# Self attention of layer 1 in steps of two units, with the transposed probabilities in the banks of the scores

## The reference

```
def cross_attention(x, ctx, wq, wk, wv, wo, bo):      # here ctx is the same layer-normed x
    q = einsum('bne,ef->bnf', x, wq).reshape(B, N, 20, 64).transpose(0, 2, 1, 3)
    k = einsum('bme,ef->bmf', ctx, wk)...; v = einsum('bme,ef->bmf', ctx, wv)...
    attn = softmax(einsum('bhnd,bhmd->bhnm', q, k) * 64 ** -0.5)
    out = einsum('bhnm,bhmd->bhnd', attn, v).transpose(0, 2, 1, 3).reshape(B, N, 1280)
    return einsum('bnf,fe->bne', out, wo) + bo
x = cross_attention(layer_norm(x, g1, be1), layer_norm(x, g1, be1), wq1, wk1, wv1, wo1, bo1) + x
```

## Time and profile before

| | us |
|---|---|
| median of 3 runs | 3640.47 (3639.7 to 3643.22) |
| the profiled execution, its own time | 3640.09 |
| its span in the trace | 3638.3 |
| self attention stage `a1`, first product to the last sum | 1145.08 to 2329.39 |

### The profile page before, as it was taken

The page is one execution under the profiler, slowest core; times in us unless marked ns, Lnnn a source line. Parts: engine busy times, 40 slices in busy tenths (PEclk is TensorE's granted clock), DMA queues, the critical chain, the costliest instruction groups (busy, mean ns, idle before and its releaser), DMA issues. The chain is left out here.

```text
span 3638.3 us, 93033 instructions
## 1 busy us (share of the span) xinstructions
PE 3565.8 (98%) x37535; PEld 3078.2 (85%) x37535; DVE 2316.8 (64%) x3902; ACT 2073.9 (57%) x5150; POOL 1255.6 (35%) x1278
## 2 busy tenths in 40 slices
PE   8999999999998999999999999799999999999999
PEld 6777787878887898989889898688888888888888
DVE  5788866664554666666667676566666666666554
ACT  5777777774335555555555555455555555555333
POOL 5333333331443333333333333322233222333432
PEclk9999999999999999999999999999999999999999
DMA  4444332322001000000000000100000000000000
GB/s 108 104 121 101 94 91 77 93 75 73 0 0 35 2 1 2 2 2 1 2 2 1 2 2 1 25 4 3 4 3 3 4 3 4 3 3 2 20 22 22
DMA packets 99740, 101.44 MB, mean 28 GB/s; under 512 B 31248, under 2 KB 74128, under 8 KB 99344
## 3 DMA queue, kind: packets, MB, share of 16 engines
q1 hardware_dynamic: 93408, 94.41, 10.2%
q0 software_dynamic: 5120, 1.35, 0.2%
q10 hardware_dynamic: 816, 0.08, 0.0%
HBM read 20.76 MB, written 5.24 MB: 7 GB/s over the span
## 5 line engine op out<-in xcount | busy, mean ns | idle before, releaser
L1250 POOL TENSOR_TENSOR a_probs<-a_probs,a_rsums 128x1024 f32<-128x1024 f32 x160 | 303.9, 1899 | 752.1 <-DVE a_rsums L1407 752.1
L1288 ACT ACTIVATE a_probs<-a_scores_banks,a_negmax 128x128 f32<-128x128 f32 x1280 | 367.4, 377 | 284.0 <-DVE a_negmax L1395 284.0
L1288 ACT ACTIVATE c_probs<-c_scores_banks,c_negmax 128x77 f32<-128x77 f32 x1280 | 317.6, 350 | 251.4 <-DVE c_negmax L1395 251.1
L1250 POOL TENSOR_TENSOR c_probs<-c_probs,c_rsums 128x616 f32<-128x616 f32 x160 | 197.8, 1236 | 729.9 <-DVE c_rsums L1407 729.9
L724 ACT ACTIVATE s_probs<-s_scoresT_banks 128x1024 f32<-128x1024 f32 (+1 forms) x320 | 327.6, 1024 | 181.4 <-PE s_scoresT_banks L901 179.2
L810 DVE TENSOR_REDUCE s_negmax<-s_scores_banks 128x8 f32<-128x1024 f32 (+1 forms) x320 | 322.4, 1007 | 135.5 <-PE s_scores_banks L883 131.3
L1388 DVE COPY a_outT<-a_out_bank 128x512 f32<-128x512 f32 x160 | 110.7, 692 | 294.2 <-PE a_out_bank L1605 239.4
L1789 DVE SCALAR_TENSOR_TENSOR f_hidden<-f_value_bank,bias,f_gate 128x512 f32<-128x512 f32 x160 | 120.1, 750 | 247.2 <-ACT f_gate L1764 245.2
L679 POOL DMA_DIRECT2D s_q_stack<-s_shift x160 | 93.8, 586 | 488.0 <-ACT s_shift L747 481.6
L1395 DVE TENSOR_REDUCE a_negmax<-a_scores_banks 128x4 f32<-128x512 f32 x320 | 206.2, 686 | 86.9 <-PE a_scores_banks L1475 86.9
L1764 ACT ACTIVATE f_gate<-f_gate_bank,bias 128x512 f32<-128x512 f32 x160 | 110.1, 688 | 260.6 <-PE f_value_bank L325 260.5
(11 more groups left out here) (306 smaller groups left out, 10405.0 us busy)
## 6 DMA issues: line engine op xcount, KB each, us to landing
s_q_stack<-front SPq DMA_DIRECT2D x192, 160.0 KB, 3.3
s_k_stack<-front SPq DMA_DIRECT2D x96, 160.0 KB, 3.8
s_out<-s_heads SPq DMA_DIRECT2D x128, 80.0 KB, 2.6
s_k_stack<-front SPq DMA_DIRECT2D x96, 96.2 KB, 2.9
x_tokens<-in_x SPq DMA_DIRECT2D x16, 320.0 KB, 3.6
out_x<-x_tokens SPq DMA_DIRECT2D x16, 320.0 KB, 2.4
s_q_stack<-s_shift POOLq DMA_DIRECT2D x160, 8.0 KB, 2.6
s_ctx_in<-in_ctx SPq DMA_DIRECT2D x16, 115.5 KB
```

Of the source, the lines that this page charges most:

```text
L1250: nc.gpsimd.tensor_tensor(probs[i][:], probs[i][:], rsums[(k - 1) % 2][:].unsqueeze(2).broadcast_to([P, UNIT, NK]), ALU.mult).then_inc(s_p ...
L1288: done = nc.scalar.activation(probs[i][:, h, :], scores[:, h // GROUP, h % GROUP * NK:(h % GROUP + 1) * NK], ACT.Exp, bias=negmax[k % 2][: ...
```

## The change

The self attention gets a builder of its own, `attention_wide_self`. Its steps are *doubles* d of two units, first = 2d and second = 2d + 1. The scores of both units are issued together, then everything that uses the full array (Y, P, V, T of both, in a fixed order), then the head outputs of both. There is a second set of score banks, and the transposed probabilities of unit n go into the banks of the scores of the same parity (those of unit n + 2, once its exponentials have been read), so that `pt` is gone; the head outputs of odd units go into `odd_bank`. `probsT` and `outT` have two buffers, `probs` four and not five. The output projection is four units behind and not three. The layer norm's transposes use `even_bank`, and its ScalarE part is split in a scaling (early in the step) and casts (at its end). Cross attention and all else stay as they were. The core of the diff (S, T and O are `scores_step`, `transpose_step` and `values_step`):

```diff
     def scalar_affine(self, e, n, par, bank, parts_used):
+        self.scalar_scale(e, n, bank)
+        self.scalar_high(e, n, par, parts_used)
+
+    def scalar_scale(self, e, n, bank):
         nc, m, t = self.m.nc, self.m, self.t
         if isinstance(n, int) and n == 0:
...
+    def scalar_high(self, e, n, par, parts_used):
+        nc, t, n = self.m.nc, self.t, n + self.offset
         e.wait_ge(t.s_y, n * 2 + 2)
...
+def attention_wide_self(m, tag, wo, context, weights, norm, following, next_norm, crossing):
...
+    T_LAG, Y_LAG = 2, 4
...
+        scores = [banks2(f"scores{i}") for i in range(2)]
+        out_bank, y_bank, even_bank, odd_bank = bank("out"), bank("y"), bank("even"), bank("odd")
...
+        probs = [sb(f"probs{i}", [P, UNIT, TOK]) for i in range(4)]
...
+        probsT = [sb(f"probsT{i}", [P, UNIT, P]) for i in range(2)]
+        outT = [sb(f"outT{i}", [P, GROUP * P]) for i in range(2)]
...
+            for d in range(-3, DOUBLES + 2):
+                step(d, 2 * d, 2 * d + 1)
+                for k in range(2 * d - LAST, 2 * d - LAST + 2):
+                    hand_over(k)
+
...
+            def step(d, first, second):
+                which, ahead, seq = transposed_at(d)
+                exponentials(first, 0, 4)
+                if which:
+                    which.scalar_scale(act, ahead, even_bank)
+                n = context_at(d)
+                if n is not None:
+                    act.wait_ge(crossing.s_T, n + 1)
+                    nc.scalar.copy(ctx_high[0:CTX_D, n * PAIR * CTX_TOK:(n + 1) * PAIR * CTX_TOK], even_bank[0:CTX_D, 0:PAIR * CTX_TOK])\
+                        .then_inc(crossing.s_high, 1)
+                exponentials(first, 4, 8)
+                tile_out(first, 0)
+                exponentials(second, 0, 1)
+                tile_out(first, 1)
+                exponentials(second, 1, 3)
+                values_out(first)
+                exponentials(second, 3, 8)
+                tile_out(second, 0)
+                tile_out(second, 1)
...
+                    nc.vector.tensor_copy(outT[n % 2][:], (out_bank, odd_bank)[n % 2][:]).then_inc(s_outT, 1)
...
+                    nc.vector.tensor_copy(probsT[n % 2][:].rearrange("p (j h) k -> p j (h k)", j=2), scores[n % 2][:]).then_inc(s_probsT, 1)
...
+            def step(d, first, second):
+                output_copy(first - Y_LAG)
+                output_copy(second - Y_LAG)
+                maxima(first)
+                maxima(second)
+                residual(first - Y_LAG)
+                which, ahead, seq = split_at(d)
+                if which:
+                    which.vector_split(dve, ahead, ahead % 2)
...
+                totals(first)
+                residual(second - Y_LAG)
...
+                transposed_copy(first - T_LAG)
+                totals(second)
+                transposed_copy(second - T_LAG)
...
+            def scores_step(n):
+
+                if not live(n, WUNITS):
+                    return
+                g = n % GROUPS
+                if due(n - 1):
+                    pe.wait_ge(s_exp, n - 1)
+                if due(n - 3):
+                    pe.wait_ge(s_probsT, n - 3)
...
+            def transpose_step(n):
+
+                if not live(n, WUNITS):
+                    return
+                pe.wait_ge(s_exp, min(n + 3, WUNITS))
+                pe.wait_ge(s_probs, n + 1)
+                if n + 2 >= WUNITS:
+                    pe.wait_ge(s_probsT, n - 1)
+                for h in range(UNIT):
+                    last = nc.tensor.transpose(scores[n % 2][:, h // GROUP, h % GROUP * P:(h % GROUP + 1) * P], probs[n % 4][:, h, :],
+                                               m.ident[:])
+                last.then_inc(s_pt, 1)
...
+                par, place = pair % 2, (out_bank, odd_bank)[n % 2]
+                pe.wait_ge(s_probsT, n + 1)
+                if due(n - 1):
+                    pe.wait_ge(s_outT, n - 1)
+                if n % 2:
+                    pe.wait_ge(s_qk, min(2 * (n + T_LAG + GROUPS) + 2, 2 * WUNITS))
...
+                if which == 0:
+                    if g == 0:
+                        pe.wait_ge(done.s_split, BASE + n + 1)
+                    if due(r):
+                        pe.wait_ge(s_v, r)
+                else:
+                    if due(r):
+                        pe.wait_ge(s_qk, 2 * r)
+                    if u % 2 == 0 and due(u - 2):
+                        pe.wait_ge(s_outT, u - 2)
...
+            def step(d, first, second):
+                scores_step(first)
+                scores_step(second)
+                which, ahead, seq = transposed_at(d)
+                n = context_at(d)
+                if which:
+                    pe.wait_ge(s_v, min(first + GROUPS, WUNITS))
...
+                    last.then_inc(crossing.s_T, 1)
+                output_step(first - Y_LAG)
+                if which or n is not None:
+                    output_step(second - Y_LAG)
+                    if which:
+                        pe.wait_ge(done.s_y, 2 * (which.offset + ahead) + 2)
+                    else:
+                        pe.wait_ge(s_ctx_split, n + 1)
+                    project(first, 0)
+                    project(first, 1)
+                else:
+                    project(first, 0)
+                    project(first, 1)
+                    output_step(second - Y_LAG)
+                project_values(first)
+                transpose_step(first - T_LAG)
+                project(second, 0)
+                project(second, 1)
+                transpose_step(second - T_LAG)
+                project_values(second)
+                values_step(first - T_LAG)
+                values_step(second - T_LAG)
+
...
-        attention_wide(m, "a1", False, L1("wo1"), context, weights[3], self_norm, weights[4], cross_norm, crossing)
+        attention_wide_self(m, "a1", L1("wo1"), context, weights[3], self_norm, weights[4], cross_norm, crossing)
```

263 lines of the change are left out of this document (added).

## The result

After takes 3593.67 us (median of 4 runs, 3591.85 to 3595.70) where before takes 3640.09 (4 runs, 3636.47 to 3643.22): ratio 0.9876, 95% interval 0.986 to 0.9891. The profiled execution's span is 3590.0 us against 3638.3, 48.3 less. The stage now lasts from 1143.71 to 2280.29, 1136.6 us where it was 1184.3: 47.7 of the 48.3.

A forecast was written before the change was run, and what follows sets the result against it. It took TensorE's order and pace, including changes of array division, as the bound. Steady part 38, start 0.5 and tail 3 made 41.5 us off 3640.47, forecasting 3599 us, range 3586 to 3616.

The forecast's parts named there:

- Six changes of division become three: Self attention's steady part: a double has three array-division changes where two units had six, saving 0.50 us a double.
- Rival 2: Price hangs on changes between float32 and split float32 products, so it only moves; time stays at 3640; chance 0.05.
- The three left cost what they cost now: Condition on the 0.50 us a double saved: the three remaining division changes keep their present price.
- Added borders: New neighbours within the double's full-array part, such as T to P: up to 0.1 us, taken as 0.03 a double.
- rival 1: ScalarE's copy of V is late in every double, by 0.2 us (3614) or 0.3 (3622); chance 0.15.
- The layout: One double's order laid out by hand; the V copy just fits, 1.02 us against 1.04 to 1.1 of cover.
- The sign given for rival 1: Load-side idle time named "ACT a_v" before the second unit's P would show the V copy coming late.
- Ten units: Steady part: ten units go from 72.2 to 69.7 us, saving 2.5; over units 2 to 153, 38 us.
- Rival 3: The round through ScalarE sets the double; at 0.8 us of wait, 24 us slower, 3662; chance 0.06.
- The start: The stage's first double takes 10.1 us where the first two units take 10.6: 0.5 us of gain.
- The tail: Unit 154's scores to the last sum, now 57.9 us: 3 us gain, between a loss of 5 and gain of 8.

The follow-up runs named there:

- e1: After, with the second unit's scores issued behind the first output projection, not beside the first unit's scores: 3649.32 us, ratio 1.0023 to before, too wide to use.
- e2: After, with the first unit's head outputs issued ahead of the double's last V and the second's behind it: 3619.56 us, ratio 0.9945 to before.
- e6: After, with both scores and head outputs of the two units split apart, new buffers and banks kept: 3653.92 us, ratio 1.0046 to before.
- e3: After, with the second unit's output projection moved behind the first unit's V in doubles without a norm: 3590.25 us, ratio 0.9877 to before.
- e8: Before, with GpSimd's subtractions for the cross stage's weights cut to 8 of 1280 columns in the self-attention tail: 3629.96 us, ratio 0.9953 to before.
- e5: Before, with 12 identity transposes a step added ahead of the head outputs in the last seven self-attention steps: 3637.32 us, ratio 0.9993 to before.

## Why the prediction was right, and where it was not

**Six changes of division become three.** Right in mechanism and nearly in size. Shown by e1, e2 and e6: two added changes cost 0.40 and 0.36 us a double, four cost 0.76, where the forecast's 0.50 for three is 0.17 a change. Rival 2 is out by e1 and e2: neither adds a change between plain and split float32 (S takes Y's place ahead of P, O takes T's ahead of V), and both cost.

**The three left cost what they cost now.** Here the term was mis-sized by a little. S is now followed by Y; there the last step of S has 0.10 and the first of Y 0.10, 0.20, where S to T had 0.16. With 0.14 and 0.20 at the other two that is 0.54 a double, not 0.50, so 0.46 was saved.

**Added borders.** I took 0.03 a double from a range of 0 to 0.1, and 0.05 for waits. The border T to P alone costs 0.10, and e3 shows that in plain doubles it is the copy of V that comes late: rival 1 in small, at half of its 0.2. The layout had 1.02 us from V's last product to the end of its copy; in the double shown above it is 1.10 (2114.51 to 2115.61), since ScalarE was still at two exponentials, and P starts 0.05 behind that, which the layout left out. The sign given for rival 1, idle time named "ACT a_v", did not appear, though the wait was there: it is too short to be named. The other new borders are at pace: V to T 0.24 in V's own step.

**Ten units, 69.7 forecast, 69.84 measured.** Plain doubles 13.72 forecast, 13.75 to 13.81 measured; norm doubles 14.27, measured 14.24 and 14.28. 2.38 us saved for 2.5, 35.5 us in all for 38. 0.46 less 0.10 is the 0.37 that a plain double saved. Rival 3 (whose 24 us make 3664 and not 3662), the round through ScalarE, did not appear: no load or product before T or S names the exponentials.

**The start.** 0.5 forecast, 1.0 measured. No run was spent on it.

**The tail.** This is the step that failed, by size: 3 us forecast, 11.2 measured, outside even its own bound of 8. The sum had it at 51 and 3.5 of clock on top, 54.5, where 46.7 came: doubles 77 and 78 took 13.5 and 11.2 us for 15.0 and 11.5, the rest 22.0 for 24.5, and nothing was lost to the clock. Two of its terms were carried over from before: VectorE's 3.29 us of weight splitting, and the low clock, which I added "the same". They are 1.7 and 3.5 of the 7.8 us; the 1.5 of double 77 was laid out too long by hand, with no run to say where. The rows of the kernel after show neither (windows above: clock 1.00). Timeline of VectorE and GpSimd after:

```profile
2257.82 1.58 DVE L321 SCALAR_TENSOR_TENSOR w_stack<-a_v,minus_last_row,staging 96x1280 fp32r<-96x1280 f32 x1 [0.64 <-ACT a_v L290]
...
2263.65 0.47 DVE L205 SCALAR_TENSOR_TENSOR pair_stack<-pair_yhigh,minus_low_row,pair_y 128x256 fp32r<-128x256 f32 x1
...
2258.02 4.14 POOL L307 TENSOR_TENSOR w_low<-staging,w_high 128x1280 fp32r<-128x1280 f32 x1
2265.79 1.90 POOL L1217 TENSOR_TENSOR a_probs<-a_probs,a_rsums 128x1024 f32<-128x1024 f32 x1 [3.63 <-DVE a_rsums L1346]
```

In the new order one of VectorE's two splits starts 0.20 us ahead of a GpSimd subtraction and the other stands where GpSimd is idle. They take 1.58 and 0.47 us where they took 3.29 and 3.10; GpSimd pays 4.14 for 2.90, and has 3.6 us to spare behind it. e8 puts a price of 8.0 us on that overlap in the kernel before; that it is worth as much in the kernel after is inferred from these rows, since no run puts the overlap back there. That the remaining 3.2 (49.9 to 46.7) come from taking the last units in pairs is what is left over, not shown by a run of its own: the 3 us that I had forecast for the whole tail.

So the total is right because 38 was 2.5 too much, and the tail and start 8.7 too little; most of that gain comes, by e8's price, from where VectorE's and GpSimd's operations came to lie, which the prediction did not look at. That part is luck. On the steady part the forecast was better than the total shows.

## What to carry to other kernels

Where products that use the array in different divisions alternate, count the changes and price them from the steps on both sides of a border, at the trace's undisturbed pace; then collect several units' products of one division, if PSUM has the banks. Lay the new order out by hand against each copy that a bank waits for, and give the tightest place one more block as cover. When an order moves, don't carry long durations of VectorE or GpSimd over to the sum before looking at what runs beside them: an operation several times as long as the same shape elsewhere may be a collision in time, and that may be gone in the new order.

## What the runs showed of the hardware

A change of division costs 0.14 to 0.21 us in these kernels (0.40 and 0.36 for two), part of it ahead of the border and part on the first step behind it, between products of one kind too. Into O it is 0.14, from S to T 0.16, O to S, Y to S and S to Y or P 0.19 to 0.20, O to V 0.21. Neighbouring groups of one division cost nothing: the second O's loads have 0.0 us of idle time.

A VectorE operation on two SBUF operands, begun while GpSimd works on SBUF, ended 0.28 us behind GpSimd's (2316.71 and 2316.43), at 3.10 us where it takes 0.47 alone. The Trainium skill, page "SBUF — State Buffer", section "Who interferes with whom", gives a rule for it: VectorE with two SBUF inputs contends with GpSimd's reads for a shared port, and issue order decides who blocks. The trace agrees where GpSimd began first (VectorE 3.10 for 0.47) and where VectorE did by 0.20 (GpSimd 4.14 for 2.90); before's first split began at 2297.37 and took 3.29 for 1.58. The GpSimd multiplication beside it began 0.06 later, but an earlier GpSimd operation was still running, timeline of the kernel before:

```profile
2296.86 0.61 POOL L149 TENSOR_TENSOR pair_h<-pair_centred,pair_rstd 128x256 f32<-128x256 f32 x1
2297.43 1.89 POOL L1250 TENSOR_TENSOR a_probs<-a_probs,a_rsums 128x1024 f32<-128x1024 f32 x1
2299.29 2.10 POOL L159 TENSOR_TENSOR x_tokens<-x_tokens,out_bias 128x320 f32<-128x320 f32 x1
```

The last of these takes 0.86 in the kernel after and 2.10 here, beside the rest of VectorE's split: first one engine waited, then the other. That VectorE found GpSimd at work when it began agrees with the rule; records 0.06 us apart would not show it alone.

TensorE's granted clock stood at 1.00, its higher level, through all of e8's tail, where before had 0.91 over its own tail and 0.85 in the end of it. The products are the same 390. Up to the first O at the lower level (2304.98) the traces differ in how long TensorE waited for VectorE: 2.30 us just before it, where e8 has 1.74. In e5, with part of that wait filled by transposes, the same O took 1.02 us, so the level had not fallen. Each of this rests on one profiled execution.
